# One tensor instead of two under the scatter-adds of a mixture-of-experts layer

## The chip, the cores and the metric

The kernel runs on one core of a Trainium2 chip, as one program. The metric is the device time of that core in microseconds: the median of three runs. The three runs of the kernel before took 5418.36, 5415.98 and 5410.62 us, so the time before is 5415.98 us.

## The reference, cut to what matters

One transformer layer on x of 4 sequences x 2048 tokens x 512 channels, in float32. Both branches read the same layernorm, and everything is summed into one output:

```
xn = layernorm(x)
# attention branch
q, k, v = split(xn @ Wqkv)
k, v = conv over groups of 4 tokens (stride 4), a learned first row put ahead
out = softmax(mask(q k^T * 512**-0.5)) @ v          # 16 heads of 32
out = out @ W_out + b_out
attn = real(fft(fft(out, axis=channels), axis=tokens))
# expert branch
shared = silu(xn @ sh_gate) * (xn @ sh_up) @ sh_down # width 1024
topk_idx, w = route(xn)          # 8 of 64 experts, out of 4 of 8 groups
routed[tok] += w * (silu(xn[tok] @ gate[e]) * (xn[tok] @ up[e])) @ down[e]   # width 256
result = x + attn + shared + routed
```

For this document the last two lines matter: the routed part is a sum over eight experts per token, gathered and added back by token, and it meets x, the shared expert and the Fourier transform of the attention in one sum.

## The kernel before, in words

The program has four stages that run one after the other, each with its own instruction lists for the engines. Engines meet at semaphores. A helper `hold` waits until a semaphore has reached a count; `then_inc` lets an instruction raise a semaphore when it (for a DMA: its data) is done. Large intermediate tensors lie in HBM and are named `t["..."]`, in the profile `mid_...`.

**Stage A** (16 steps of 512 tokens): layernorm, projections, routing scores. SP (SyncE) issues all its stores from one ordered list. `xn` is stored for the gathers of the experts. Into one step's list, `clear(s)` at L332 (defined at L352) puts one store that fills 512 rows of `t["base1"]` with zeros from a zeroed tile `spare`. Ahead of the steps SP stores 128 pad rows to `xn`, `base0` and `base1`, and a tile `blank` to `ids`, the list of slots: its first column holds token numbers, and an iota on GpSimd fills it with pad rows (8192 and on), so that slots which no token takes point at pad rows. At the end of the stage SP waits until all stores have landed.

**Stage B**: attention, and the shared expert. `store_x` (L978) writes x + shared to `t["base0"]`. GpSimd scatters token numbers and weights to `ids`, sorted by expert in blocks of 256 slots (`RB`), each block of one expert, two halves (`RT` = 2) of 128 rows. About 278 blocks are needed for the data given.

**Stage E** walks these blocks. For each block b:
- GpSimd copies the block's 2 x 128 token numbers (L1739) and issues two indirect DMAs that gather rows of `xn` into `xg` (L1742), for the block four ahead of the adds' block in its list. It waits first until PE has transposed the block that held the buffer (`t_filled`).
- PE transposes the gathered rows (L1931), multiplies by gate and up weights (L1944) and by down weights (L1956). Each float32 product is three products of split values, high and low.
- ACT (ScalarE) makes the high halves (`wgu_hi` L1788, for the gate and up weights), DVE (VectorE) subtracts them to get the low halves: L1865 over 128x2048 and, right behind it, L1870 over 128x1024.
- ACT and DVE bring the result, weighted, into `rows`. GpSimd waits for it (`y_emptied`), copies the token numbers once more (L1749), and issues two indirect DMAs that add 128 rows each to HBM (L1754): the first half of the block onto `t["base0"]`, the second onto `t["base1"]`.

A token may stand in several blocks, so an add may read and write a row that an earlier add is still writing. Within one half this can't be (an expert takes a token once). Across blocks a wait keeps order: the add of half i waits until the add of half i of the previous block has landed. The two halves go to different tensors and don't wait for each other:

```python
for i in range(RT):
    if not first:
        hold(pool, added[i], b * 16, passed)
    pool.indirect_dma_start(t[f"base{i}"], ..., rows[s][:, i, :], None, compute_op=ALU.add).then_inc(added[i], 16)
```

Both waits stand on GpSimd, which issues in order; behind the adds of a block stand the next copy and the next gathers. At the end of the stage a barrier waits for all of it. An object `ahead` uses spare time of the stage to prepare the first folds of the next.

**Stage C**: the Fourier transform. The attention is folded (differences and sums of mirrored rows), projected on PE (L2173) and transformed over tokens in 32 units n of 128 rows and their 128 mirrored rows. PE makes a unit's products (L2206, L2209), ACT and DVE combine them into `dif` and `turned` (L2284 to L2289), and `turn_rows` (L2192) turns rows around on PE for the mirrored ones. Then DVE adds the unit's rows of x + shared + routed: `rows_up` (L2291, L2293) and `rows_down` (L2297). These rows come by `load_rows` (L2079) into a ring of six cells of 128 x 2048: four loads of 256 KB each, the up and down rows from `base0` and from `base1`. GpSimd adds the two (L2147) and lets DVE go on with `base_ready`. Four middle rows, one per sequence, are loaded from both tensors and added by GpSimd in its list behind the seventh unit (L2151). SP stores the up and down rows to the output and then loads the unit that takes the cell next, `load_rows(n - 1 + RING)`. Only the last four units' stores and a short tail (L2218, L2219 on PE) stand behind the last turn.

Of the kernel before, what the change touches and what calls it, by code (L numbers as in the profile page):

```python
# [11 lines left out]
ALU = mybir.AluOpType  # L12
# [3 lines left out]
P = 128  # L16
# [147 lines left out]
def stage_a(nc, t, early):  # L164
    ctx = ExitStack()
    with ctx:
# [118 lines left out]
        def _(sp):  # L285
# [35 lines left out]
            def step(s, ahead, last):  # L321
# [10 lines left out]
                clear(s)  # L332
# [36 lines left out]
            sp.wait_ge(spare_out, 16 * (4 + NSTEP))  # L369
# [389 lines left out]
def stage_b(nc, t, early):  # L759
    ctx = ExitStack()  # L760
    with ctx:
# [163 lines left out]
        def _(sp):  # L925
# [45 lines left out]
            def load_x(s):  # L971
                rows = slice(s % NSTEP * TB, (s % NSTEP + 1) * TB)
                if s:
                    sp.wait_ge(base_out, 16 * s)
                sp.dma_start(x[:, :, :], t["x" if s < NSTEP else "base0"][rows, :].rearrange("(i p) c -> p i c", p=P))\
                    .then_inc(x_in, 16)

            def store_x(s):  # L978
                rows = slice(s % NSTEP * TB, (s % NSTEP + 1) * TB)
                sp.wait_ge(y_emptied, TPB * (s + 1))  # L980
                sp.dma_start(t["base0"][rows, :].rearrange("(i p) c -> p i c", p=P), x[:, :, :]).then_inc(base_out, 16)
# [625 lines left out]
def stage_e(nc, t, ahead):  # L1607
    ctx = ExitStack()
    with ctx:
# [123 lines left out]
        def _(pool):  # L1733
# [12 lines left out]
            def add_rows(b, s, after, first=False):  # L1746
# [3 lines left out]
                hold(pool, ox_ready, after * 2 + s + 9, passed)  # L1750
                for i in range(RT):
                    if not first:
                        hold(pool, added[i], b * 16, passed)
                    pool.indirect_dma_start(t[f"base{i}"], bass.IndirectOffsetOnAxis(ap=ox[s][:, i:i + 1], axis=0),  # L1754
# [234 lines left out]
def stage_c(nc, t, ahead):  # L1989
    ctx = ExitStack()  # L1990
    with ctx:
# [6 lines left out]
        RING = 6  # L1998
# [39 lines left out]
        rows_in = [sem(f"rows_in{e}") for e in range(RING)]  # L2038
        base_ready = sem("base_ready")
        up_ready = sem("up_ready")  # L2040
        out_ready = sem("out_ready")
        out_done = [sem(f"out_done{e}") for e in range(RING)]
        last_in = sem("last_in")
        last_summed = sem("last_summed")
# [19 lines left out]

        def up(n):
            return cell[n % RING][:, 0:DIM]

        def down(n):
            return cell[n % RING][:, DIM:2 * DIM]

        @block.sync
        def _(sp):
# [6 lines left out]
            def load_rows(n):  # L2079
                e = n % RING  # L2080
                rows, a, b = unit(n)
                if n < RING:
                    last_att = max(i for i in range(NATT) if i % RING == e)
                    sp.wait_ge(d_ready, last_att + 1)
                else:
                    sp.wait_ge(out_done[e], stored(e, n // RING))
# [18 lines left out]
            for n in range(RING):  # L2105
# [8 lines left out]
            for b in range(BATCH):  # L2114
                row = b * SEQ + MID_ROW
                for i, src in enumerate((t["base0"], t["base1"])):
                    sp.dma_start(last[0:1, i * BATCH + b, :], src[row:row + 1, :]).then_inc(last_in, 16)
            for n in range(NU_):
                rows, a, b = unit(n)
                e = n % RING  # L2120
# [11 lines left out]
                if n and n - 1 + RING < NU_:  # L2132
                    load_rows(n - 1 + RING)
# [4 lines left out]
            for e in range(RING):  # L2138
                sp.wait_ge(out_done[e], stored(e, len(range(e, NU_, RING))))
            sp.wait_ge(last_done, 16 * BATCH)  # L2140

# [263 lines left out]
```

## Time and profile before

| | |
|---|---|
| device time of the three runs | 5418.36, 5415.98, 5410.62 us |
| median | 5415.98 us |
| profiled execution, span | 5418.5 us, the one time that is given for it |
| PE (TensorE matmul) busy | 5303.0 us, 98% |
| PEld (TensorE weight load) busy | 4440.9 us, 82% |
| DVE busy | 3828.9 us, 71% |
| ACT busy | 2615.1 us, 48% |
| POOL (GpSimd) busy | 3028.9 us, 56% |

The shares are means over stages with different limits. A busy PE is not a PE at its peak, since its matmuls are pipelined and their ends are modelled. The profile's times are counted from the span's start; stage E lies between about 2490 and 5130 us in them, the transform behind it. In the rows of the section on the trace a line "A <- B: us, times, longest" is a wait of A that B ended; in a timeline each line begins with a start and a duration in us, and ends with the idle time of the engine ahead of it and what released it.

### The profile page before, as it was taken

How to read it: one execution, taken by the hardware profiler on the slowest of the kernel's cores; microseconds unless marked ns; L12 is line 12 of the kernel's file. 1: busy time of each engine (PE TensorE's matmuls, PEld its weight loads, DVE VectorE, ACT ScalarE, POOL GpSimd, SP SyncE). 2: the span in 40 equal slices, each digit the busy share in tenths (PEclk: the TensorE clock that was granted, in tenths of full speed). 3: DMA queues.
4: the chain of work that ended last, by engine and by line, in shares of the span. 5: the costliest groups of instructions: out<-in, count | busy, mean ns of one | idle time of the engine just before them, and what ended most of it. 6: DMA issues, size and time to landing. Idle time of an engine off the chain costs nothing. (4 is left out here: it accounts for less than half of the span.)

```text
span 5418.5 us, 102292 instructions
## 1 busy us (share of the span) xinstructions
PE 5303.0 (98%) x32880; PEld 4440.9 (82%) x32880; DVE 3828.9 (71%) x7311; ACT 2615.1 (48%) x3833; POOL 3028.9 (56%) x2716
## 2 busy tenths in 40 slices
PE   8999989999999999998999999999999999999999
PEld 6888866766666667667999999989999999999786
DVE  6666667778787877775676666766667666666664
ACT  3333333333343333335666666666666666666410
POOL 1222215666666665115777777777777777777514
PEclk9999989999999999998999999999999999999999
DMA  7777764444454444435676677767787676676748
GB/s 239 248 242 255 250 173 129 133 134 119 136 148 135 119 141 118 134 98 119 134 158 112 134 170 150 163 132 167 158 227 158 135 164 129 134 156 113 178 154 289
DMA packets 500414, 864.75 MB, mean 160 GB/s; under 512 B 64388, under 2 KB 165493, under 8 KB 497694
## 3 DMA queue, kind: packets, MB, share of 16 engines
q1 hardware_dynamic: 356014, 567.12, 33.2%
q0 software_dynamic: 140928, 292.13, 29.5%
q10 hardware_dynamic: 3312, 3.47, 0.3%
q8 instruction: 88, 1.44, 0.1%
q14 instruction: 72, 0.59, 0.0%
HBM read 498.49 MB, written 330.47 MB: 153 GB/s over the span
## 5 line engine op out<-in xcount | busy, mean ns | idle before, releaser
L1754 POOL DMA_INDIRECT mid_base<-e_rows,e_ox x556 | 1160.3, 2087 | 372.5 <-POOL e_ox L1749 239.5
L1865 DVE TENSOR_TENSOR e_wgu_lo<-e_wgu,e_wgu_hi 128x2048 fp32r<-128x2048 f32 x278 | 637.5, 2293 | 806.4 <-ACT e_wgu_hi L1788 676.6
L1742 POOL DMA_INDIRECT e_xg<-mid_xn,e_ix x556 | 625.5, 1125 | 336.4 <-POOL e_ix L1739 226.4
L1801 ACT CAST e_xT_hi<-e_ps_t 128x512 fp32r<-128x512 f32 x556 | 299.1, 590 | 929.8 <-PE e_ps_t L1931 929.8
L1069 POOL DMA_INDIRECT mid_ids<-b_pairs,b_cell x512 | 614.3, 1200 | 141.8 <-issue 141.0
L1944 PE MATMUL e_ps_g<-e_xT_hi,e_wgu_hi 128*128 128x256 f32 x2224 | 652.9, 294 | 1.7 <-issue 1.7
L1944 PE MATMUL e_ps_g<-e_xT_lo,e_wgu_hi 128*128 128x256 f32 x2224 | 630.0, 283 | 0.0
L1944 PE MATMUL e_ps_g<-e_xT_hi,e_wgu_lo 128*128 128x256 f32 x2224 | 629.7, 283 | 0.0
L1944 PE MATMUL e_ps_u<-e_xT_hi,e_wgu_hi 128*128 128x256 f32 x2224 | 629.4, 283 | 0.0
L1944 PE MATMUL e_ps_u<-e_xT_lo,e_wgu_hi 128*128 128x256 f32 x2224 | 629.4, 283 | 0.0
L1944 PE MATMUL e_ps_u<-e_xT_hi,e_wgu_lo 128*128 128x256 f32 x2224 | 629.4, 283 | 0.0
L1197 DVE CUSTOM_DVE_ANT_0 b_ps_s<-b_ps_s,ab_mask,ab_s_null 128x32 f32<-128x32 f32 (+15 forms) x1024 | 460.3, 490 | 130.0 <-PE b_ps_s L1417 123.7
L1788 ACT CAST e_wgu_hi<-e_wgu 128x2048 fp32r<-128x2048 f32 x278 | 531.4, 1912 | 23.1 <-DMA e_wgu<-in_up_w 23.1
L1062 POOL TENSOR_SCALAR_AFFINE_SELECT b_p_diag<-b_p_diag 128x512 f32<-128x512 f32 x256 | 160.2, 650 | 537.4 <-ACT b_p_diag L1120 537.4
L1956 PE MATMUL e_ps_y<-e_wd_hi,e_hT_hi 128*128 128x512 f32 x1112 | 436.2, 392 | 0.0
L1956 PE MATMUL e_ps_y<-e_wd_lo,e_hT_hi 128*128 128x512 f32 x1112 | 436.0, 392 | 0.0
L1956 PE MATMUL e_ps_y<-e_wd_hi,e_hT_lo 128*128 128x512 f32 x1112 | 433.6, 390 | 0.0
L1944 PEld LDWEIGHTS e_ps_g<-e_xT_hi,e_wgu_hi 128*128 128x128 f32 x2224 | 426.4, 192 | 2.1 <-issue 2.1
L1944 PEld LDWEIGHTS e_ps_g<-e_xT_lo,e_wgu_hi 128*128 128x128 f32 x2224 | 427.9, 192 | 0.0
L1944 PEld LDWEIGHTS e_ps_u<-e_xT_lo,e_wgu_hi 128*128 128x128 f32 x2224 | 427.0, 192 | 0.0
L1944 PEld LDWEIGHTS e_ps_u<-e_xT_hi,e_wgu_lo 128*128 128x128 f32 x2224 | 427.0, 192 | 0.0
L1944 PEld LDWEIGHTS e_ps_g<-e_xT_hi,e_wgu_lo 128*128 128x128 f32 x2224 | 427.0, 192 | 0.0
(286 smaller groups left out, 13368.0 us busy)
## 6 DMA issues: line engine op xcount, KB each, us to landing
b_xT_hi<-mid_xT_hi SPq DMA_DIRECT2D x32, 1024.0 KB
b_xT_lo<-mid_xT_lo SPq DMA_DIRECT2D x32, 1024.0 KB
mid_base<-b_x SPq DMA_DIRECT2D x32, 1024.0 KB
e_wgu<-in_gate_w SPq DMA_DIRECT2D x62, 512.0 KB
e_wgu<-in_up_w SPq DMA_DIRECT2D x62, 512.0 KB
e_wd<-in_down_w SPq DMA_DIRECT2D x62, 512.0 KB
ec_cell<-mid_base SPq DMA_DIRECT2D x88, 256.0 KB, 4.9
ab_q<-mid_q_hi SPq DMA_DIRECT2D x82, 256.0 KB, 4.0
```

The costliest lines, as they stand in the source:

```text
L1062: pool.affine_select(p_diag[:, h, :], p_diag[:, h, :], [[1, QC]], ALU.is_ge, 0.0, base=1 - CF, channel_multiplier=-CF).then_inc(masked, 1)
L1069: pool.indirect_dma_start(t["ids"], bass.IndirectOffsetOnAxis(ap=cell[r][:, i:i + 1], axis=0), pairs[r][:, i, :], None).then_inc(scattered ...
L1197: dve.tensor_tensor_reduce(S[:, 0:w_], S[:, 0:w_], mask[:, NC - w_:NC], 1.0, null_of(u)[:, qt, h:h + 1], ALU.add, ALU.max, mx[:, qt, h:h + ...
L1742: pool.indirect_dma_start(xg[s][:, i, :], None, t["xn"], bass.IndirectOffsetOnAxis(ap=ix[s][:, i:i + 1], axis=0))\
L1754: pool.indirect_dma_start(t[f"base{i}"], bass.IndirectOffsetOnAxis(ap=ox[s][:, i:i + 1], axis=0), rows[s][:, i, :], None, compute_op=ALU.a ...
L1788: act.copy(wgu_hi[s][:, :], wgu[s][:, :]).then_inc(gu_hi_ready, 1)
L1801: act.copy(xT_hi[s][:, i * DC // 2 * RB:(i + 1) * DC // 2 * RB], ps_t[i][:, :]).then_inc(xT_hi_ready, 1)
L1865: dve.tensor_tensor(wgu_lo[s][:, :], wgu[s][:, :], wgu_hi[s][:, :].bitcast(F32), ALU.subtract)\
L1944: last = pe.matmul(dst[s][:, h * RB:(h + 1) * RB], w[s][:, w0:w0 + P], x[s][:, x0:x0 + RB], start=k == 0 and n == 0, stop=k == DC - 1 and ...
L1956: last = pe.matmul(ps_y[i][:, :], x[s][:, h0:h0 + P], w[s][:, h * DIM:(h + 1) * DIM], start=h == 0 and n == 0, stop=h == HC - 1 and n == 2)
```

## The change

`base0` and `base1` become one tensor `base`. Both halves of a block are added onto it, and the transform loads it alone. What belongs to that:

- The store of x + shared goes to `base`. `base1`, its clears in stage A (`clear`) and its pad rows are gone.
- `xn` and `base` have 256 pad rows (`RB`) in place of 128, filled by one store each of 256 rows, and the iota gives each slot of a block a pad row of its own (before, the two halves of a block used the same 128).
- In stage E an add waits for the landing of both adds of the previous block: both holds stand ahead of the two adds.
- In stage C one load for the up rows and one for the down rows of a unit are left; the four sums of middle rows and all of GpSimd's sums are gone, with their semaphores. DVE waits for the loads (`rows_in`, `last_in`) themselves. A half-cell holds one unit, so that the ring is twelve units long (`URING`); `home(n)` gives a unit its half-cell, in the order in which the cells come free from the folds.

```diff
@@ stage A, SP
-                clear(s)
...
-            for dst in (t["xn"], t["base0"]):
-                sp.dma_start(dst[TOK:TOK + P, :], spare[:, :]).then_inc(spare_out, 16)
-
-            def clear(s):
-                sp.dma_start(t["base1"][bass.ds(s * TB, TB), :].rearrange("(i p) c -> p i c", p=P),
-                             spare[:, None, :].broadcast_to([P, TPB, DIM])).then_inc(spare_out, 16)
-
-            sp.dma_start(t["base1"][TOK:TOK + P, :], spare[:, :]).then_inc(spare_out, 16)
+            for dst in (t["xn"], t["base"]):
+                sp.dma_start(dst[TOK:TOK + RB, :].rearrange("(i p) c -> p i c", p=P),
+                             spare[:, None, :].broadcast_to([P, RT, DIM])).then_inc(spare_out, 16)
...
-            pool.iota(blank[:, :, 0], pattern=[[0, NCOL]], base=TOK, channel_multiplier=1).then_inc(blank_ready, 1)
+            pool.iota(blank[:, :, 0].rearrange("p (b i) -> p b i", i=RT), pattern=[[0, NBLK], [P, RT]], base=TOK,
+                      channel_multiplier=1).then_inc(blank_ready, 1)
@@ stage E, GpSimd: add_rows
+                if not first:
+                    for i in range(RT):
+                        hold(pool, added[i], b * 16, passed)
                 for i in range(RT):
-                    if not first:
-                        hold(pool, added[i], b * 16, passed)
-                    pool.indirect_dma_start(t[f"base{i}"], ...
+                    pool.indirect_dma_start(t["base"], ...
@@ stage C
-        RING = 6
+        RING, URING = 6, 12
...
+        def home(n):
+            e = n % URING
+            return (e // 2 + (NATT - RING) % RING) % RING, e % 2 * 2 * DIM
...
             def load_rows(n):
-                if n < RING:
-                    last_att = max(i for i in range(NATT) if i % RING == e)
-                    sp.wait_ge(d_ready, last_att + 1)
+                if n < URING:
+                    sp.wait_ge(d_ready, NATT - RING + n // 2 + 1)
                 else:
...
-                for i, src in enumerate((t["base0"], t["base1"])):
-                    o = i * 2 * DIM
-                    sp.dma_start(cell[e][:, o:o + DIM], src[a, :]).then_inc(rows_in[e], 16)
-                    sp.dma_start(cell[e][:, o + DIM:o + 2 * DIM], src[b, :]).then_inc(rows_in[e], 16)
+                sp.dma_start(up(n), t["base"][a, :]).then_inc(rows_in[e], 16)
+                sp.dma_start(down(n), t["base"][b, :]).then_inc(rows_in[e], 16)
...
-        @block.gpsimd
-        def _(pool):
-            for n in range(NU_):
-                e = n % RING
-                pool.wait_ge(rows_in[e], 64 * (n // RING + 1))
-                pool.tensor_tensor(cell[e][:, 0:2 * DIM], cell[e][:, 0:2 * DIM], cell[e][:, 2 * DIM:4 * DIM], ALU.add)\
-                    .then_inc(base_ready, 1)
-                if n == RING:
-                    pool.wait_ge(last_in, 16 * 2 * BATCH)
-                    pool.tensor_tensor(last[:, 0:BATCH, :], last[:, 0:BATCH, :], last[:, BATCH:2 * BATCH, :], ALU.add)\
-                        .then_inc(last_summed, 1)
...
-                dve.wait_ge(base_ready, n + 1)
+                dve.wait_ge(rows_in[n % URING], 32 * (n // URING + 1))
...
-            dve.wait_ge(last_summed, 1)
+            dve.wait_ge(last_in, 16 * BATCH)
```

## Rows read from the trace of the kernel before

**Rows 1.** Stretches of 100 us, stage E, and the columns.
```profile
core 0: us, PE busy (x) PEld busy (x) DVE busy (x) ACT busy (x) POOL busy (x), PEclk, DMA share, GB/s
3540.00:3640.00 100.00, 95.70 (x684) 88.10 (x684) 66.17 (x71) 60.47 (x82) 74.19 (x63) 1.00 0.64 122
4000.00:4100.00 100.00, 100.00 (x732) 94.51 (x731) 68.35 (x76) 66.32 (x88) 71.46 (x64) 1.00 0.87 216
```

**Rows 2.** Waits of PE over the span: total us, times, longest.
```profile
PE e_ps_t L1931 <- DMA e_xg<-mid_xn,e_ix: 36.9, 16, 25.6
...
PE b_ps_s L1417 <- SPq L999: 10.9, 1, 10.9
PE a_bank L732 <- DMA a_wraw<-a_ks: 9.3, 2, 7.3
...
PE c_bank L2173 <- PEq L1609: 7.6, 1, 7.6
```

**Rows 3.** Timeline of GpSimd and PE, steady stretch of stage E.
```profile
5062.04 2.07 POOL L1754 DMA_INDIRECT mid_base<-e_rows,e_ox  x1 [0.30 <-issue]
...
5066.51 1.25 POOL L1742 DMA_INDIRECT e_xg<-mid_xn,e_ix  x1 [0.31 <-issue]
...
5068.95 1.63 POOL L1754 DMA_INDIRECT mid_base<-e_rows,e_ox  x1 [0.99 <-POOL e_ox L1749]
5070.88 2.56 POOL L1754 DMA_INDIRECT mid_base<-e_rows,e_ox  x1 [0.30 <-issue]
...
5072.36 1.03 PE L1931 MATMUL e_ps_t<-e_ident,e_xg 128*128 128x128 f32 x8
```

**Rows 4.** Timeline of DVE, the same stretch.
```profile
5069.69 2.29 DVE L1865 TENSOR_TENSOR e_wgu_lo<-e_wgu,e_wgu_hi 128x2048 fp32r<-128x2048 f32 x1 [2.79 <-ACT e_wgu_hi L1788]
5071.90 1.22 DVE L1870 TENSOR_TENSOR e_wd_lo<-e_wd,e_wd_hi 128x1024 fp32r<-128x1024 f32 x1
```

**Rows 5.** Timeline of DVE and GpSimd about 3516 us, stage E.
```profile
3516.12 2.29 DVE L1865 TENSOR_TENSOR e_wgu_lo<-e_wgu,e_wgu_hi 128x2048 fp32r<-128x2048 f32 x1 [2.79 <-ACT e_wgu_hi L1788]
3516.71 3.19 POOL L1754 DMA_INDIRECT mid_base<-e_rows,e_ox  x1 [1.00 <-DMA mid_base<-e_rows,e_ox]
...
3520.21 1.57 POOL L1754 DMA_INDIRECT mid_base<-e_rows,e_ox  x1 [0.31 <-PE e_ps_t L1931]
```

**Rows 6.** First line of the page.
```profile
span 5418.5 us, 102292 instructions
```

**Rows 7.** A stretch of 10 us at the end of stage A.
```profile
700.00:710.00 10.00, 0.00 (x0) 0.00 (x0) 2.54 (x3) 0.12 (x1) 2.54 (x2) 0.70 0.83 297
```

**Rows 8.** Timeline of GpSimd, the end of stage E: its adds.
```profile
5097.24 2.23 POOL L1754 DMA_INDIRECT mid_base<-e_rows,e_ox  x1 [0.94 <-POOL e_ox L1749]
...
5101.96 1.88 POOL L1754 DMA_INDIRECT mid_base<-e_rows,e_ox  x1 [2.49 <-DMA mid_base<-e_rows,e_ox]
...
5112.02 1.68 POOL L1754 DMA_INDIRECT mid_base<-e_rows,e_ox  x1 [2.12 <-DMA mid_base<-e_rows,e_ox]
...
5117.77 1.55 POOL L1754 DMA_INDIRECT mid_base<-e_rows,e_ox  x1 [1.37 <-DMA mid_base<-e_rows,e_ox]
```

**Rows 9.** Waits of GpSimd between 2490 and 5095 us.
```profile
POOL mid_base L1754 <- DMA mid_base<-e_rows,e_ox: 21.9, 22, 1.2
```

**Rows 10.** Timeline of DVE, PE and GpSimd, the first units of the transform.
```profile
5263.89 0.42 DVE L2291 TENSOR_TENSOR ec_cell<-ec_cell,c_dif 128x257 f32<-128x257 f32 x1
...
5266.72 1.02 PE L2192 MATMUL c_bank<-c_turned,c_flip 128*128 128x512 f32 x2
...
5270.05 4.57 POOL L2151 TENSOR_TENSOR ec_fold<-ec_fold 1x2048 f32<-1x2048 f32 x1
5270.17 7.03 DVE L2291 TENSOR_TENSOR c_cell<-c_cell,c_dif 128x257 f32<-128x257 f32 x1
5271.03 1.02 PE L2192 MATMUL c_bank<-c_turned,c_flip 128*128 128x512 f32 x2
...
5286.21 1.02 PE L2192 MATMUL c_bank<-c_turned,c_flip 128*128 128x512 f32 x2
```

More of the change, by code:

```diff
@@ L368, in _ @@
             sp.wait_ge(cnt_out, 16)
-            sp.wait_ge(spare_out, 16 * (4 + NSTEP))
+            sp.wait_ge(spare_out, 16 * 3)
             sp.wait_ge(early.loaded, 16 * 14)
@@ L974, in load_x @@
                     sp.wait_ge(base_out, 16 * s)
-                sp.dma_start(x[:, :, :], t["x" if s < NSTEP else "base0"][rows, :].rearrange("(i p) c -> p i c", p=P))\
+                sp.dma_start(x[:, :, :], t["x" if s < NSTEP else "base"][rows, :].rearrange("(i p) c -> p i c", p=P))\
                     .then_inc(x_in, 16)
@@ L980, in store_x @@
                 sp.wait_ge(y_emptied, TPB * (s + 1))
-                sp.dma_start(t["base0"][rows, :].rearrange("(i p) c -> p i c", p=P), x[:, :, :]).then_inc(base_out, 16)
+                sp.dma_start(t["base"][rows, :].rearrange("(i p) c -> p i c", p=P), x[:, :, :]).then_inc(base_out, 16)
             def store_att(u):
@@ L2037, in stage_c @@
         r_filled = sem("r_filled")
-        rows_in = [sem(f"rows_in{e}") for e in range(RING)]
-        base_ready = sem("base_ready")
+        rows_in = [sem(f"rows_in{e}") for e in range(URING)]
         up_ready = sem("up_ready")
         out_ready = sem("out_ready")
-        out_done = [sem(f"out_done{e}") for e in range(RING)]
+        out_done = [sem(f"out_done{e}") for e in range(URING)]
         last_in = sem("last_in")
-        last_summed = sem("last_summed")
         last_filled = sem("last_filled")
@@ L2063, in stored @@
             return 32 * rounds + (16 if e < BATCH else 0)
+        def home(n):
+            e = n % URING
+            return (e // 2 + (NATT - RING) % RING) % RING, e % 2 * 2 * DIM
         def up(n):
-            return cell[n % RING][:, 0:DIM]
+            c, o = home(n)
+            return cell[c][:, o:o + DIM]
         def down(n):
-            return cell[n % RING][:, DIM:2 * DIM]
+            c, o = home(n)
+            return cell[c][:, o + DIM:o + 2 * DIM]
         @block.sync
@@ L2104, in _ @@
                 load_att(i)
-            for n in range(RING):
+            for n in range(URING):
                 load_rows(n)
@@ L2115, in _ @@
                 row = b * SEQ + MID_ROW
-                for i, src in enumerate((t["base0"], t["base1"])):
-                    sp.dma_start(last[0:1, i * BATCH + b, :], src[row:row + 1, :]).then_inc(last_in, 16)
+                sp.dma_start(last[0:1, b, :], t["base"][row:row + 1, :]).then_inc(last_in, 16)
             for n in range(NU_):
                 rows, a, b = unit(n)
-                e = n % RING
+                e = n % URING
                 sp.wait_ge(up_ready, n + 1)
@@ L2131, in _ @@
                     sp.dma_start(t["out"][hi, :], down(n)[most:rows, :]).then_inc(out_done[e], 16)
-                if n and n - 1 + RING < NU_:
-                    load_rows(n - 1 + RING)
+                if n and n - 1 + URING < NU_:
+                    load_rows(n - 1 + URING)
             sp.wait_ge(last_ready, 1)
@@ L2137, in _ @@
                 sp.dma_start(t["out"][row:row + 1, :], last[0:1, b, :]).then_inc(last_done, 16)
-            for e in range(RING):
-                sp.wait_ge(out_done[e], stored(e, len(range(e, NU_, RING))))
+            for e in range(URING):
+                sp.wait_ge(out_done[e], stored(e, len(range(e, NU_, URING))))
             sp.wait_ge(last_done, 16 * BATCH)
-        @block.gpsimd
-        def _(pool):
-            for n in range(NU_):
-                e = n % RING
-                pool.wait_ge(rows_in[e], 64 * (n // RING + 1))
-                pool.tensor_tensor(cell[e][:, 0:2 * DIM], cell[e][:, 0:2 * DIM], cell[e][:, 2 * DIM:4 * DIM], ALU.add)\
-                    .then_inc(base_ready, 1)
-                if n == RING:
-                    pool.wait_ge(last_in, 16 * 2 * BATCH)
-                    pool.tensor_tensor(last[:, 0:BATCH, :], last[:, 0:BATCH, :], last[:, BATCH:2 * BATCH, :], ALU.add)\
-                        .then_inc(last_summed, 1)
         @block.tensor
```

9 lines of the change are left out of this document (5 added, 4 removed).

## The prediction

> **What bounds the kernel now.** I read the page's first line, then the stretch table, the waits of PE, GpSimd's timeline beside VectorE's in one stretch of the expert stage, its late stretch and its end, and last the stretch of the transform where PE stood still. The reader is to see that PE sets the time nearly everywhere: in a normal 100 us of the expert stage it is busy 100.00 us and issues 732 instructions [rows 1], and its waits are few [rows 2]. So only a change that lengthens or shortens one of those waits counts. Four of the places are touched by the edit: the end of stage A, the gathers of stage E (36.9 us in 16 waits, of which 25.6 is the stage's first gather, so 11.3 us in 15), the barrier at the end of stage E (7.6 us), and the transform.
>
> In stage E the engine to watch is GpSimd. It issues two gathers, a copy and two adds per block, and the adds share its time with VectorE's two weight splits (L1865, L1870). The second add starts at 5070.88 inside that pair (5069.69 to 5073.12) and takes 2.56 us; the first starts at 5068.95, 0.74 us ahead of the pair, and takes 1.63 [rows 3, 4]. When a first add does start inside the pair (3516.71, the pair began at 3516.12) it takes 3.19 us and the second follows at 3520.21, 3.50 us behind instead of 1.93 [rows 5]. After that event PE issued 684 instructions in 100 us instead of 732 [rows 1]: 48 of 732, so 6.6 us of the 100 were lost, because GpSimd was late and the gathers with it. That is a cliff 0.74 us wide, and the edit pushes toward it.
>
> **The change part by part.** The sum is made against the profiled execution, span 5418.5 us [rows 6]; nothing beside the span is given for it. The median of the three runs is 5415.98, 2.5 us below.
>
> *Stage A.* Sixteen 1 MB clears go, and one pad store of three; the two left are twice as long. Between the first and last step PE waits for no transfer (both L732 waits stand in the first and the last step [rows 2]), so fourteen clears are hidden already: 0. In the first step 0.26 MB more stands in the queue ahead of the next x, about 0.9 us at the 297 GB/s of the draining queue [rows 7], and one issue fewer on SP works the other way: 0, between -0.9 and +0.9. At the end of the stage the queue is being drained with PE at 0.00 busy, 297 GB/s [rows 7]; 1.05 MB less is worth up to 3.5 us, but the small stores of the last step are issued only after that step's last results and land behind them whatever is ahead. I take 0.7, nearer the end where issue decides; bounds 0 and 3.5. The new iota pattern fills the same tile and is done long before SP asks for it: 0.
>
> *Stage E, each block.* Before, a first add waited for the previous block's first add, which had been issued 1.93 us ahead of the second. Now it waits for the second too. Behind it on GpSimd stand its own pair, the next index copy and the next two gathers; for these PE waits. How much room is there? At the quiet end of the stage an add started at 5112.02 and the one that waited for its landing started at 5117.77: 5.75 us, with 1.68 for the issue itself [rows 8]. In the steady stretch the second add is issued in 2.07 us, so the earliest start behind it is 5.75 + 0.39 = 6.14; the next first add started 6.91 us behind it (5062.04 to 5068.95) [rows 3]. Room: 0.77 us, and 0.74 more to the cliff. So a quiet block pays nothing. A block whose landing is over 1.5 us late runs into the splits and is then 3 us late.
>
> How many are there? GpSimd's waits for an add that ended with a landing are 22 between 2490 and 5095 us [rows 9]: in each the *first* add, the one with the most room, landed only as the new one was about to start, most of a block behind its issue. Read along the timeline they stand in about 15 places, since neighbours come together. The second add, behind it on the same queue, lands later still, so I count each place as one fall over the cliff: 15. A place costs at least 0 (a gather is issued 5.85 us ahead of its transposes, 5066.51 and 5072.36 [rows 3], so that 3 us late leaves half the lead, and most of the 22 waits cost PE little today) and at most what the one visible event cost, 6.6 us: 0 to 99 us. The nearest row is that of the gather waits, 11.3/15 = 0.75 us each [rows 2]; a late GpSimd meets about two of them before it is back in step. 15 x 1.5 = 22.5 us.
>
> One rule speaks against this term. The Trainium skill (SBUF — State Buffer, "Who interferes with whom") says that a tensor_tensor with both inputs in SBUF takes only the shared pair's read interface, while descriptor generation needs the write interface, which it marks as inferred. L1865 and L1870 are such instructions, so by that rule an add that starts inside them costs no more than one outside, the cliff is gone, and the term of 22.5 is near 0. The 3.19 us of that event [rows 5] disagree; the time by the rule is that of the first rival.
>
> *Stage E, the end.* The last blocks' adds are already a chain of landings: 5101.96, 5112.02, 5117.77 [rows 8], and PE stands for 7.6 us at the barrier behind them [rows 2]. Now the first add of the block at 5097.24 can start only where its second one starts today, 5101.96, and its second comes one add (1.93 [rows 3]) behind. The same repeats at the next two blocks. 3 x 1.93 = 5.8 us, all on the path. Bounds: 0 (if the landings get shorter by what is added, as the queue empties) and 7.6 (three times an add of 2.23 and a gap of 0.30 [rows 3, 8]).
>
> *Stage C.* SP issues half as many loads of rows and GpSimd adds nothing. Turns of PE come every 4.31 us here (5266.72, 5271.03); two later one is due at 5279.65 and came at 5286.21, 6.56 us late [rows 10]. The reader is to see why: VectorE's L2291, 0.42 us otherwise, took 7.03 from 5270.17, while GpSimd summed the middle rows (5270.05) and a unit on either side. Its operands had been there for long, so it was not a late load, and the longer ring by itself is worth 0; the sums' going is worth the 6.6. No other unit of the transform loses a turn, and the next thing that could be late, a load for the thirteenth unit, has a dozen units' time. Bounds: 5.0 to 7.0. Halved loads in the rest of the stage are hidden behind PE: 0.
>
> Sum: 5418.5 - 0.7 + 22.5 + 5.8 - 6.6 = 5439.5, and 2.5 lower for the median: **5437 us**.
>
> **The rivals.** *The landings are absorbed* (not slower). GpSimd's lead swallows each late block, or the splits don't hold back an add. Place: the first add of each block; price 0 in place of 22.5; it decides if first adds stay under 2 us. 5437 - 22.5 = 5414.5, since the end of E and C cancel. For it: most late landings cost little today. Against: today's holds are on the add with more room.
>
> *The stage stays late.* Once over the cliff GpSimd does not fall back in step, and half or all places cost 6.6 us: 7.5 x 6.6 = 49.5 or 99 in place of 22.5: 5464 to 5513. For it: the one event [rows 5] lasted over a hundred us. Against: it did end by itself.
>
> *The relief is larger* (faster). No cliff, landings at E's end shorter by what is added (0 for 5.8), and the full 3.5 at the end of A: 5414.5 - 5.8 - 2.8 = 5406, a little lower with the first step's 0.9.
>
> **How the numbers follow.** Forecast 0.46 (its own range 5425 to 5455), absorbed 0.30, stays late 0.12, larger relief 0.12, of which 0.09 lies under 5405. About 0.2%, 10.8 us, is what a measurement of this kernel can tell from no change. Slower: forecast and stays late, 0.58. Same: absorbed and what is left of the relief, 0.33. Faster: 0.09. The range leaves out nine in a hundred at the bottom and the longer half of the late case at the top: 5406 to 5472.
>
> **What would show it.** Stage E: waits of an add for a landing well above 22, first adds of over 3 us in a dozen places, PE's waits for gathers up from 36.9 us by 15 to 30, and stretches with fewer than 732 PE instructions in 100 us. If first adds stay at 1.6 us and the gather waits at 37 us, that term is wrong. The end of E: PE's wait at the barrier 13 us in place of 7.6. Stage C: no turn late, L2291 at 0.42 throughout. Stage A: PE's wait into stage B shorter than 10.9 us [rows 2] by under 2. The forecast is wrong if E's pace is untouched, or if a stall in C is left.

## The result and the profile after

The changed kernel takes 5482.89 us (median of four runs, 5468.08 to 5488.83) against 5417.17 for the kernel before, with one more run than is shown above: a ratio of 1.0117, 95% interval 1.0105 to 1.0129. It is 65.7 us slower. The forecast was 5437 with a range to 5472: the sign was right, the size a third of what came, and the time lies where the rival "the stage stays late" had put it, to which 0.12 was given.

The profiled execution is 67.2 us longer than that of before [rows 6]:

```profile
span 5485.7 us, 102149 instructions
```

From PE's first and last instruction of each stage: the transposes of stage E begin at 2470.0 us in place of 2473.3, and the stage lasts 2718.1 in place of 2644.9 (73.2 more); from its end to the first projection 11.5 in place of 7.6; the transform takes 279.6 in place of 285.9. In sum -3.3 + 73.2 + 3.9 - 6.3 = 67.5 (behind PE's last instruction 0.3 is won). Nearly all of it is stage E.

PE's waits after, the rows that answer [rows 2] (total us, times, longest):

```profile
PE e_ps_t L1928 <- DMA e_xg<-mid_xn,e_ix: 85.2, 49, 24.2
...
PE c_bank L2159 <- PEq L1605: 11.6, 1, 11.6
...
PE b_ps_s L1413 <- SPq L995: 9.4, 1, 9.4
```

The waits for gathers rose from 36.9 us in 16 to 85.2 in 49. GpSimd's waits between 2490 and 5160 us, the answer to [rows 9]:

```profile
POOL mid_base L1751 <- DMA mid_base<-e_rows,e_ox: 116.5, 61, 3.7
```

The rows count all of the engine's idle time ahead of an add, if a landing ended it. About a microsecond of that stands between the copy and a first add in any block (0.99 us in the median before, 1.09 after, with two waits). Beyond it, landings held first adds for 50 us after, and for 0.2 us before. How one such wait reaches PE is seen in GpSimd's timeline about 3520 us (start, duration; idle time ahead and its releaser in brackets):

```profile
3520.18 3.43 POOL L1751 DMA_INDIRECT mid_base<-e_rows,e_ox  x1 [2.67 <-DMA mid_base<-e_rows,e_ox]
3523.92 1.59 POOL L1751 DMA_INDIRECT mid_base<-e_rows,e_ox  x1 [0.30 <-PE e_ps_t L1928]
...
3526.58 1.02 POOL L1738 DMA_INDIRECT e_xg<-mid_xn,e_ix  x1 [0.87 <-POOL e_ix L1735]
3527.90 0.98 POOL L1738 DMA_INDIRECT e_xg<-mid_xn,e_ix  x1 [0.30 <-issue]
```

and in PE's, with the stretches around it (PE busy, PEld, DVE, ACT, POOL, clock, DMA share, GB/s):

```profile
3535.52 1.32 PE L1928 MATMUL e_ps_t<-e_ident,e_xg 128*128 128x128 f32 x8 [3.02 <-DMA e_xg<-mid_xn,e_ix]
```

```profile
3534.00:3536.00 2.00, 0.48 (x4) 0.48 (x5) 0.00 (x0) 0.00 (x0) 1.14 (x3) 1.00 1.05 179
3536.00:3538.00 2.00, 2.00 (x13) 2.00 (x12) 1.10 (x2) 1.71 (x4) 1.70 (x2) 0.56 1.03 247
3538.00:3540.00 2.00, 2.00 (x12) 2.00 (x12) 0.79 (x2) 2.00 (x4) 0.41 (x2) 0.59 1.05 301
3540.00:3542.00 2.00, 2.00 (x19) 2.00 (x18) 0.08 (x1) 2.00 (x3) 0.00 (x0) 1.00 1.08 400
```

The add waits 2.67 us (1.09 of them stand there anyway), starts inside the splits and takes 3.43; the gathers behind it are issued three microseconds late, PE stands for 3.02 us, and then its granted clock is near the lower of its two levels (1.2 of 2.4 GHz) for some four microseconds, with 12 or 13 matmuls in two microseconds; in the two behind them, at full clock, it is 19.

The second way is a state that lasts. GpSimd and VectorE in it, about 2930 us:

```profile
2929.47 1.02 POOL L1738 DMA_INDIRECT e_xg<-mid_xn,e_ix  x1 [0.86 <-POOL e_ix L1735]
2930.79 0.99 POOL L1738 DMA_INDIRECT e_xg<-mid_xn,e_ix  x1 [0.30 <-issue]
2931.79 2.05 POOL L1745 COPY e_ox<-e_ids 128x2 int32 x1
2934.92 1.63 POOL L1751 DMA_INDIRECT mid_base<-e_rows,e_ox  x1 [1.09 <-issue]
```

```profile
2931.51 2.29 DVE L1862 TENSOR_TENSOR e_wgu_lo<-e_wgu,e_wgu_hi 128x2048 fp32r<-128x2048 f32 x1 [3.02 <-ACT e_wgu_hi L1785]
2933.71 1.22 DVE L1867 TENSOR_TENSOR e_wd_lo<-e_wd,e_wd_hi 128x1024 fp32r<-128x1024 f32 x1
```

No landing is waited for here. The copy of two row numbers, 0.19 us otherwise, starts inside the first split and takes 2.05, to that split's end; the add follows 1.09 us behind it. Now GpSimd waits for no other engine: from 2929.47 to the same gather of the next block, 2939.51, it is 10.04 us, and the next time, with a copy of 1.38, 9.46. Both are more than the 9.38 that PE needs. So it does not come back in step. From about the 40th to the 70th block the stage ran this way, with blocks of 9.43 and about 10.1 us in turn, and 100 us of it read so, beside the 732 of [rows 1]:

```profile
2930.00:3030.00 100.00, 95.34 (x684) 87.82 (x683) 65.55 (x70) 60.11 (x81) 72.89 (x62) 1.00 0.65 126
```

The distances of PE's transposes tell what each way costs. The 61 blocks in which a copy was held for over 1 us are 39.7 us longer than 9.38 in sum, against 6.3 for the 12 such blocks before; all other blocks are 50.7 us longer, against 12.1. So of the 72 us that blocks grew by, the lasting state has 33 and blocks without a held copy, as the one at 3520 us, have 39.

For contrast, a block in step, where an add starts inside the splits too and it costs PE nothing (no copy is held, the gathers keep their lead):

```profile
2628.48 0.19 POOL L1745 COPY e_ox<-e_ids 128x2 int32 x1
2629.77 2.78 POOL L1751 DMA_INDIRECT mid_base<-e_rows,e_ox  x1 [1.09 <-issue]
```

### The profile page after: what moved, and what is told of

Same layout as the page of the kernel before. It is cut to its first block and busy times, and to the rows that moved or that the text cites. A ratio compares the mean times of both kernels' runs of the same rounds, so it can differ in the third digit from the quotient of the medians.

```text
span 5485.7 us, 102149 instructions
## 1 busy us (share of the span) xinstructions
PE 5316.7 (97%) x32880; PEld 4443.4 (81%) x32880; DVE 3815.8 (70%) x7311; ACT 2604.1 (47%) x3833; POOL 2939.1 (54%) x2683
## 5 line engine op out<-in xcount | busy, mean ns | idle before, releaser
L1751 POOL DMA_INDIRECT mid_base<-e_rows,e_ox x556 | 1109.6, 1996 | 450.2 <-issue 293.6
L1738 POOL DMA_INDIRECT e_xg<-mid_xn,e_ix x556 | 590.1, 1061 | 336.3 <-POOL e_ix L1735 226.4
L1941 PEld LDWEIGHTS e_ps_u<-e_xT_hi,e_wgu_hi 128*128 128x128 f32 x2224 | 427.2, 192 | 0.0
```

What stands on the lines that cost most here:

```text
L1738: pool.indirect_dma_start(xg[s][:, i, :], None, t["xn"], bass.IndirectOffsetOnAxis(ap=ix[s][:, i:i + 1], axis=0))\
L1751: pool.indirect_dma_start(t["base"], bass.IndirectOffsetOnAxis(ap=ox[s][:, i:i + 1], axis=0), rows[s][:, i, :], None, compute_op=ALU.add). ...
L1941: last = pe.matmul(dst[s][:, h * RB:(h + 1) * RB], w[s][:, w0:w0 + P], x[s][:, x0:x0 + RB], start=k == 0 and n == 0, stop=k == DC - 1 and ...
```

## The experiments

Times are medians, in runs beside the kernel before on the same chip. "Longer blocks" is the sum over blocks 3 to 276 of what the distance from a block's first transpose to the next one's is above 9.38 us: 18.3 us before, 90.4 after. "Waits for gathers" are PE's, in us; some 24 to 26 of each are the stage's first gather.

| kernel | us | ratio to before, 95% | longer blocks | waits for gathers |
|---|---|---|---|---|
| changed | 5482.89 | 1.0105 to 1.0129 | 90.4 | 85.2 |
| before + both waits | 5502.22 | 1.0086 to 1.0163 | 107.3 | 96.8 |
| changed, splits cut | 5473.66 | 1.0074 to 1.0108 | 74.5 | 33.7 |
| before, splits cut | 5482.20 | 1.0103 to 1.0134 | 82.5 | 24.5 |
| changed, copy ahead | 5448.58 | 1.0034 to 1.0066 | 50.7 | 59.0 |
| blocks in turn | 5418.89 | 0.9995 to 1.0013 | 18.6 | 36.8 |
| before, splits swapped | 5556.34 | 1.0233 to 1.0278 | 146.0 | 130.3 |
| changed, splits swapped | 5674.43 | 1.0460 to 1.0499 | 275.7 | 223.8 |

**The wait alone.** The kernel before, with nothing but the second wait:

```diff
-                for i in range(RT):
-                    if not first:
+                if not first:
+                    for i in range(RT):
                         hold(pool, added[i], b * 16, passed)
+                for i in range(RT):
                     pool.indirect_dma_start(t[f"base{i}"], ...
```

> The kernel before (two tensors, clears, GpSimd's sums, all as it was) with one edit: the first add of a block waits for both adds of the previous block. Theory A, the wait does it: a late landing of the second add puts GpSimd behind, its copies and adds fall into VectorE's two splits, and it stays behind. Then stage E loses the same 73 us and its end 4, and nothing is won back in the transform or in stage A: 5417 + 73 + 4 = 5494 us, range 5475 to 5510; PE's waits for gathers 75 to 95 us, index copies over 1 us in 40 or more blocks. Theory B, one tensor does it (adds of both halves onto one tensor land later): here the halves still go to two tensors, so the time stays at 5410 to 5430 us and the gather waits at 30 to 45 us.

Measured 5502.22 us. PE's and GpSimd's waits:

```profile
PE e_ps_t L1932 <- DMA e_xg<-mid_xn,e_ix: 96.8, 67, 23.9
...
PE c_bank L2174 <- PEq L1609: 11.6, 1, 11.6
```

```profile
POOL mid_base L1755 <- DMA mid_base<-e_rows,e_ox: 125.4, 63, 4.7
```

The time lies in the range of theory A. All of the loss in stage E (2734.5 us in the profiled execution, 2644.9 before) and the longer barrier (11.6) are there with two tensors. The wait does it; the one tensor is not needed for it.

**Without the wait, on one tensor.** The converse, as near as the order of adds allows: even blocks are added onto one tensor, odd ones onto the other, both halves of a block together.

```diff
+                if not first:
+                    hold(pool, added[s], turn * 32, passed)
                 for i in range(RT):
-                    if not first:
-                        hold(pool, added[i], b * 16, passed)
-                    pool.indirect_dma_start(t[f"base{i}"], ...).then_inc(added[i], 16)
+                    pool.indirect_dma_start(t[f"base{s}"], ...).then_inc(added[s], 16)
```

with 256 pad rows and the iota of the change, and ScalarE's waits for `added` to match.

> The kernel before, with both halves of a block added onto one tensor as in the change, but the blocks in turn: even blocks onto the one tensor, odd blocks onto the other, each with 256 pad rows. An add then waits for the adds of the block two before. Clears, sums and loads of the transform are as before. Theory A, the wait for the block just before is all that costs: the wait is gone, GpSimd waits for a landing nowhere in the steady stage, index copies over 1 us fall below the 12 of before, PE's gather waits are near the first one alone (25 to 30 us), and the 17 us by which the blocks of before are longer than 9.38 go for the most part: 5395 to 5412 us. Theory B, two halves on one tensor hinder each other: the time is above the one before, 5430 to 5490 us.

Measured 5418.89 us, no difference from before and in neither range. Two halves of a block on one tensor cost nothing that can be told. No add waits for a landing any more and no copy takes over 1 us, as theory A had it. The surprise is what stayed: PE's waits for gathers are as long as before.

```profile
PE e_ps_t L1932 <- DMA e_xg<-mid_xn,e_ix: 36.8, 21, 23.9
```

Here 12.9 us in 20 waits stand beside the first gather, where no add waits for a landing. So most of the 11.3 us of before [rows 2] does not come from late landings (3.8 of it stand in the one event of [rows 5]), and neither does most of the 18 us of longer blocks (6.3 of them in that event); the expected gain was not there.

**The splits cut.** The changed kernel, and then the kernel before, with the two splits in six pieces:

```diff
-                dve.tensor_tensor(wgu_lo[s][:, :], wgu[s][:, :], ..., ALU.subtract).then_inc(gu_lo_ready, 1)
+                for q in range(4):
+                    c = slice(q * 512, (q + 1) * 512)
+                    last_i = dve.tensor_tensor(wgu_lo[s][:, c], wgu[s][:, c], ..., ALU.subtract)
+                last_i.then_inc(gu_lo_ready, 1)
...  wd_lo in two pieces likewise
```

> The changed kernel with VectorE's splits cut: the 128x2048 subtraction in four of 512 columns, the 128x1024 one in two. Theory A, GpSimd is held back by the splits: it gets in between two pieces, a copy or an add is held for 0.6 us at most instead of up to 3.4, GpSimd falls back in step within a few blocks after a late landing; index copies over 1 us fall from 61 to under 15, 5415 to 5440 us. Theory B, the waits for landings alone (116 us of GpSimd's time in 61 waits) do it, whatever VectorE does: 5470 to 5490 us. If the time stays and copies and adds inside the pieces are still 2 to 3 us long, the pieces follow each other too closely to let GpSimd in, and the run decides nothing.

> The kernel before with VectorE's two splits cut in six pieces of 512 columns, as was tried on the changed kernel. Theory A, the pace of a block is set by a ring of ScalarE and VectorE as much as by PE, and each cut lengthens it by 0.065 us: blocks of 9.62 to 9.66 us instead of 9.38, 5417 + 72 - 10 = 5479 us, range 5470 to 5490. Theory B, that cost came from GpSimd's new wait: here there is none, 5405 to 5420 us.

Measured 5473.66 and 5482.20. Of the first expectation the time fits theory B, the trace theory A: GpSimd is never late, and the 278 copies take 0.187 us in the mean, none over 1 us.

```profile
L1745 POOL COPY e_ox<-e_ids 128x2 int32 (+1 forms) x278 | 52.1, 187 | 242.1 <-ACT e_rows L1816 242.0
```

But the wait that this run was to test is hardly met in it: between 2490 and 5145 us an add's wait ended with a landing 8 times, 9.1 us in sum, nearly all of it the microsecond that stands there anyway. The kernel before shows why. The issue of 245 of its 278 second adds took over 2.3 us (2.56 in the median); with the splits cut the median is 1.58 and one takes over 2.3. The second adds then land 4.9 us after their start in the median instead of 5.5, and 3 of 278 land too late for the next first add instead of 42 (the section on the prediction tells how this is counted). So the splits also hold back the second add, and make its landing late. What a late landing would cost beside cut splits, no run shows.

What the cut costs shows in the kernel before, where nothing waits anew: its time is in the range of theory A, and its blocks take 9.68 us in the median instead of 9.38 (in sum 82.5 - 18.3 = 64 us, since the irregular ones are gone). The pieces are 0.29 us longer in sum than the two splits [rows 4],

```profile
4505.21 2.52 DVE L1867 TENSOR_TENSOR e_wgu_lo<-e_wgu,e_wgu_hi 128x512 fp32r<-128x512 f32 x4 [2.88 <-ACT e_wgu_hi L1788]
4507.66 1.28 DVE L1874 TENSOR_TENSOR e_wd_lo<-e_wd,e_wd_hi 128x512 fp32r<-128x512 f32 x2
```

and the median block grows by as much, as if the ring of ScalarE and VectorE had no room; the ring itself was not followed. Of the two, the changed kernel has the shorter stage E (2703.1 us against 2710.4), with blocks of 9.63 us in the median against 9.68, though PE waits 8.0 us for gathers behind the first one there and 0.2 us here. Why its blocks are the shorter ones stays open.

**The copy ahead.** The changed kernel with the row numbers copied before the gathers of the same turn, away from the splits:

```diff
+                    copy_rows(i * 2 + s, s)
                     gather(i * 2 + s + 4, s, False)
                     add_rows(...)      # without its copy
```

> The changed kernel with the copy of an add's row numbers moved ahead of the gathers of the same turn, away from the splits. Theory A: in the late state GpSimd's own chain of a block is about 10.0 us against PE's 9.38, of which the held copy is 1.4 to 2.0 us; without it the chain is under 9.38, GpSimd catches up after each late landing, and of the 73 us a half or more goes: 5425 to 5455 us. Theory B, waits for landings alone: the landings and the room ahead of them are as before, 5470 to 5490 us.

Measured 5448.58: 34 of the 66 us come back, though adds wait for landings no less than in the changed kernel.

```profile
POOL mid_base L1755 <- DMA mid_base<-e_rows,e_ox: 120.3, 67, 5.9
```

14.7 us of these, in 3 waits, stand at the end of the stage. In the other 64 waits 0.50 us stands there anyway, so that landings hold adds for 73.6 us, against 50 in the changed kernel. This is the run against "the waits alone": longer waits, half the loss. Two things changed at once, though. No copy is held for over 1 us any more (each takes 0.77 us where it now stands), and from the end of a second add to the next first add it is 4.17 us in the median, 4.96 in the changed kernel. The 50.7 us of longer blocks that are left are as many as the changed kernel has in blocks without a held copy.

**The splits swapped.** VectorE's order of the two splits changed, first in the kernel before and in the changed one, then in the one with the copy ahead and with blocks in turn:

```diff
-                split_gu(b + 1, 1 - s)
                 split_d(b, s)
+                split_gu(b + 1, 1 - s)
```

> The kernel before with VectorE's two splits in the other order: the 128x1024 one (L1870), whose input is ready two us earlier, ahead of the 128x2048 one, in the time in which VectorE waits for ScalarE. Theory A, PE sets 9.38 us of a block and the ring of ScalarE and VectorE stands just below it: the ring is 1.2 us shorter, blocks stay at 9.38, of the 18 us by which some blocks are longer a part goes: 5400 to 5415 us. Theory B, the ring sets the pace: blocks fall below 9.38, 5330 to 5395 us.

> The changed kernel with the two splits in the other order. Theory A, a late landing costs what it does because the two splits in one piece (3.44 us) hold GpSimd's copy and adds back: with them apart (1.2 and 2.3 us, a gap between) GpSimd's chain in the late state falls below 9.38 and it comes back in step; most of the 73 us goes, 5408 to 5435 us. Theory B, only what lengthens the block (as cut pieces did) hides the late landings: the time stays at 5465 to 5490 us.

> The changed kernel with the splits in the other order and the copy of an add's row numbers ahead of the gathers. Theory A: both shorten GpSimd's chain in the late state; the time is at or below that with the swap alone, 5405 to 5425 us. Theory B, the copy alone is worth its 34 us and the swap nothing: 5440 to 5455 us.

> Blocks in turn on two tensors, VectorE summing the middle rows, and the splits in the other order. Theory A: no add waits for a block just before, the transform is 280 us, and the gathers are issued earlier for want of held adds: 5390 to 5408 us, below the kernel before. Theory B, the 18 us of longer blocks have to do neither with adds nor with splits: 5408 to 5416 us as without the swap.

Measured 5556.34, 5674.43, 5460.92 (1.0071 to 1.0098) and 5561.80 us (1.0254 to 1.0282). Every expectation here missed, and the misses teach most. In the kernel before with the splits swapped, GpSimd, then VectorE, then PE:

```profile
4506.04 1.68 POOL L1742 DMA_INDIRECT e_xg<-mid_xn,e_ix  x1 [0.30 <-issue]
4507.72 2.07 POOL L1749 COPY e_ox<-e_ids 128x2 int32 x1
4510.78 1.62 POOL L1754 DMA_INDIRECT mid_base<-e_rows,e_ox  x1 [0.99 <-POOL e_ox L1749]
...
4515.34 1.74 POOL L1742 DMA_INDIRECT e_xg<-mid_xn,e_ix  x1 [0.85 <-POOL e_ix L1739]
4517.38 2.53 POOL L1742 DMA_INDIRECT e_xg<-mid_xn,e_ix  x1 [0.30 <-issue]
```

```profile
4505.65 1.23 DVE L1870 TENSOR_TENSOR e_wd_lo<-e_wd,e_wd_hi 128x1024 fp32r<-128x1024 f32 x1 [1.23 <-ACT e_wd_hi L1794]
4507.45 2.29 DVE L1865 TENSOR_TENSOR e_wgu_lo<-e_wgu,e_wgu_hi 128x2048 fp32r<-128x2048 f32 x1 [0.58 <-ACT e_wgu_hi L1788]
...
4514.95 1.23 DVE L1870 TENSOR_TENSOR e_wd_lo<-e_wd,e_wd_hi 128x1024 fp32r<-128x1024 f32 x1 [1.19 <-ACT e_wd_hi L1794]
4516.75 2.29 DVE L1865 TENSOR_TENSOR e_wgu_lo<-e_wgu,e_wgu_hi 128x2048 fp32r<-128x2048 f32 x1 [0.57 <-ACT e_wgu_hi L1788]
```

```profile
4524.17 1.39 PE L1931 MATMUL e_ps_t<-e_ident,e_xg 128*128 128x128 f32 x8 [4.04 <-DMA e_xg<-mid_xn,e_ix]
```

The small split now stands where the second gather is issued (1.68 us instead of 1), and the copy behind it falls into the large one (2.07). In the next turn both gathers start inside the splits and are held themselves (1.74 and 2.53), PE stands for 4.04 us, and two blocks later all is in step again. This comes from an instruction order alone, in a kernel with the old waits. It is not the lasting state of the changed kernel: blocks with a copy held for over 1 us are longer by only 15 us in sum here. What PE stands for are held gathers: 35 took over 2 us (one before, none in the changed kernel), and 33 of PE's 36 stands of over 1.5 us come right behind one. With blocks in turn, where no add waits for a landing at all, it is 2.7% in place of 2.6, with 41 such gathers. So a late landing is only one thing that pushes GpSimd's instructions into the splits; where they fall is what is paid for. With the copy out of the way the swapped changed kernel has four such gathers and is back at 5461.

**The transform.** GpSimd's sum of the middle rows moved behind the 21st unit (`n == 20`) in the kernel before; the ring of the changed kernel set to six (`URING = 6`); and, with blocks in turn, VectorE taking that sum over behind the ninth unit:

> The kernel before with GpSimd's sum of the middle rows behind the 21st unit's sum instead of the 7th. Theory A, that sum (one partition, 2048 elements, 4.57 us) between two unit sums holds VectorE out: the 7 us L2291 leaves 5270 us and stands near the 21st unit (some 14 turns of 4.31 later, about 5330 us), and the transform is as long as before, 286 us. Theory B, the stall at 5270 us comes from the loads of the seventh unit, the first that waits for a cell of the ring: it stays where it was.

> The changed kernel with the ring of half-cells six units long instead of twelve. Theory A, the longer ring is worth nothing and the sums' going was all: the transform takes 279 to 280 us as in the changed kernel. Theory B, the ring gave the gain: it takes 284 to 286 us, with a late turn near the seventh unit.

> The kernel of blocks in turn, and VectorE instead of GpSimd sums the middle rows, behind the ninth unit. Theory A, that sum on GpSimd between two unit sums is what held VectorE out: the transform falls from 286 to 280 us, as in the changed kernel, 5389 to 5406 us. Theory B, the unit sums on GpSimd or the four loads of a unit cost as well: it stays at 283 us or above.

The stall moved with the sum,

```profile
5337.18 4.88 DVE L2291 TENSOR_TENSOR ec_cell<-ec_cell,c_dif 128x257 f32<-128x257 f32 x1
```

shorter there, and the transform took 283.0 us in place of 285.9 (one execution, 5411.12 us). With a ring of six it took 279.2 (one execution, 5488.95 us): the ring is worth nothing. With the sum on VectorE it took 279.7, though GpSimd still makes all 32 unit sums: the one sum was the whole gain. But the stall itself is only about half of the 6 us. With blocks in turn and the sum still on GpSimd, the same addition (L2292 there) took the same 7.03 us and the transform 282.8. The difference is the granted clock behind PE's stand, before and then with blocks in turn:

```profile
5275.00:5285.00 10.00, 6.45 (x16) 4.23 (x15) 7.40 (x15) 0.37 (x1) 1.92 (x1) 0.66 0.54 172
```

```profile
5271.00:5281.00 10.00, 6.42 (x27) 4.86 (x27) 8.32 (x20) 0.74 (x2) 1.70 (x2) 1.00 0.58 181
```

PE stood for some 3.6 us in both; before, its clock then was 0.66 in the mean of these 10 us, in the other 1.00. So the sum costs 3.1 us (282.8 to 279.7), and a low clock behind it another 3.1 in the execution of before. The kernel with the sum on VectorE takes 5413.42, a ratio of 0.9981 to 0.9999: the only one whose interval lies below the kernel before, by 0.1%.

**What is left of the longer blocks.** The copy ahead in the kernel before, and with blocks in turn and VectorE's sum:

> Blocks in turn on two tensors, VectorE summing the middle rows (5413 us), and the copy of an add's row numbers ahead of the gathers. Theory A, the 18 us by which blocks of the kernel before are longer than 9.38, and PE's gather waits of 11 to 13 us behind the first one, come from GpSimd's adds and copies that the splits hold back: the copy ahead frees one microsecond or more of GpSimd's chain, the adds start earlier and the rest goes: 5393 to 5406 us. Theory B, those waits come from late gathers themselves (their own landings): 5409 to 5416 us.

> The kernel before with the copy of an add's row numbers ahead of the gathers, nothing else. Theory A as for the other run: 5398 to 5412 us, blocks longer than 9.38 by less than 10 us in sum. Theory B: 5413 to 5420 us. If the add that now starts earlier only meets its landing wait more often, the gain is lost again and the time is as before.

Measured 5417.77 (0.9990 to 1.0008) and 5421.91 (0.9997 to 1.0015), with 24.5 and 24.0 us of longer blocks. GpSimd's chain is shorter there (in the second kernel 4.05 us in the median from the end of a second add to the next first add, 4.85 before), and it takes nothing off them. What they come from (the gathers' own landings remain as a candidate) stays open.

## Why the prediction was wrong, step by step

*Where to look.* Right: the four places were the four that moved, and the mechanism of stage E (a wait for the second add, GpSimd late, an add inside the splits, late gathers) is what the trace shows at 3520 us and what the run with the wait alone shows by itself.

*Stage E, the term of 22.5 us: mis-sized, 73.2 measured.* Two steps of it failed.

The count: "about 15 places ... The second add, behind it on the same queue, lands later still, so I count each place as one fall over the cliff". A wait of the *first* add was taken as the sign of a late second one. The trace of before had the thing itself, in its records of DMA packets: 256 packets of 2048 bytes per block of adds. With the end of a block's last one as its landing, the second add landed 5.53 us after its start in the median, but in 42 of 278 blocks later than the next first add could bear (1.15 us ahead of its start, the distance at which adds of the changed kernel follow a landing), and in 31 of them by more than the 0.74 us to the cliff. That is twice the 15. In another execution of the same stage (the run with the late sum) it is 31 and 20, so the count is no fixed number, but above 15 in both. The landings themselves did not get longer: the median after is 5.26, the 95th percentile 7.68, before 7.96.

The price: "the nearest row is that of the gather waits, 11.3/15 = 0.75 us each; a late GpSimd meets about two of them before it is back in step". Most of those waits have nothing to do with late landings, as the run with blocks in turn showed. By the 31 of before the price is 73.2/31 = 2.4 us per late block; it is the sum of three things. PE's waits for gathers rose by 48.3 us. The granted clock, read in stretches of 20 us from 2500 to 5100, was short of full by 16.0 us in sum (20 us times what is missing to 1.00) against 1.8 before: it fell after some of PE's longer stands, as at 3536 us. The other 11 us are not placed one by one.

In the price, "is back in step" was an error of its own. The prediction looked for adds held to 3.19 us; only 9 first adds took over 3 us; 70 took 2.3 to 3 us, 37 of these at no cost in their own or the next two blocks, as the one at 2629.77. What keeps GpSimd late is the *copy* ahead of the add: 61 copies took over 1 us, 12 before, 76 us more in sum (150.2 against 74.2). The copy was named as standing behind the wait and given no price. That is 33 of the 72 us by which blocks grew. The other 39 are in blocks without a held copy, and they too cost more than was put down: the stand at 3532 us and the low clock behind it made two blocks 3.2 and 1.6 us longer, 4.8 for one late block in place of 1.5.

The rival "the stage stays late" had the right time, 5464 to 5513, from [rows 5], in part by luck, since under half of the loss is the state that lasts. What spoke against it, that the state "did end by itself", was true and no argument: with more pushes it is entered again. The range did not do what its text says either: it ends at 5472, and the middle of that rival is 5488, so that it left out most of it and not the longer half.

*The rule of the Trainium skill.* (SBUF — State Buffer, "Who interferes with whom".) Its part that a VectorE instruction with two SBUF inputs contends with a GpSimd instruction that reads SBUF agrees with the held copies. By its inference that descriptor generation is spared, the prediction's rival had adds inside the splits cost nothing, and that is not so here: first adds that started inside the splits took 2.78 and 3.43 us, and with the splits cut none took over 1.70. Whether the inference itself is wrong stays open. An indirect add also reads its row numbers from SBUF (`ox`), which the first part of the rule would hold back, and no run separates the two.

*The end of stage E.* 5.8 us forecast, 3.9 measured; the barrier wait "13 us in place of 7.6" is 11.6. The chain of landings is as drawn, with the adds now in pairs:

```profile
5171.57 2.20 POOL L1751 DMA_INDIRECT mid_base<-e_rows,e_ox  x1 [5.86 <-DMA mid_base<-e_rows,e_ox]
...
5181.30 1.98 POOL L1751 DMA_INDIRECT mid_base<-e_rows,e_ox  x1 [4.59 <-DMA mid_base<-e_rows,e_ox]
...
5189.43 1.55 POOL L1751 DMA_INDIRECT mid_base<-e_rows,e_ox  x1 [4.10 <-DMA mid_base<-e_rows,e_ox]
```

*The transform.* 6.6 forecast, 6.3 measured. The stall was named rightly: none is left, and the 32 first additions (L2291 before) take 0.42 us throughout. That the size came out is in part luck: the 6.56 us by which the later turn was late are PE's stand of 3.55 us and turns at a lower clock behind it, and the prediction put all of it to the sums. With blocks in turn the same stall cost 3.1.

```profile
L2277 DVE TENSOR_TENSOR ec_cell<-ec_cell,c_dif 128x257 f32<-128x257 f32 x20 | 8.4, 420 | 0.0
...
L2277 DVE TENSOR_TENSOR c_cell<-c_cell,c_dif 128x257 f32<-128x257 f32 x12 | 5.0, 420 | 0.0
```

*Stage A.* 0.7 forecast. PE's wait into stage B fell by 1.5 us, 10.9 to 9.4, within the two that were named; but kernels whose stage A is untouched began stage E at 2468.3 (the wait alone) and 2469.3 (splits swapped), so the 3.3 us by which it began earlier are no sign of the clears. Nor is the wait: it is 9.4 us with the wait alone too, whose stage A is that of before.

With 73.2 in place of 22.5 and 3.9 in place of 5.8, the same sum gives 5418.5 - 0.7 + 73.2 + 3.9 - 6.6 = 5488.3 for the profiled execution, which took 5485.7.

## What to carry to other kernels

Where an engine in the side line has little room in each period, price a new wait by what happens when it is missed: follow the late engine's own chain once around with the hold-ups that it meets there, and if that is longer than the period, the lateness stays. Count how often the *new* condition would have been late from the records of that transfer, not from the waits for another one. Look whether what holds up the late engine also makes the transfer late: then a run that takes it away tests neither alone. A clean test of such a cause is the wait alone in the old kernel, and the new data path without the wait.

## What was not expected of the hardware

A GpSimd copy of 128x2 integers, 0.19 us, took up to 2.17 us beside VectorE's subtraction of two SBUF tensors, and ended with it. Between two subtractions GpSimd got in, also between pieces of 0.69 us; six pieces are 0.29 us longer than two, and here the median block grew by 0.30. In the same way gathers that started inside the splits took up to 2.53 us to issue in the lines above, not 1. And PE's stand of 3.02 us was followed by four microseconds at a granted clock of 0.56 to 0.59, so that its price is the stand and 1.8 us more (a mean clock of 0.91 over the 20 us from 3520).
